# One product with four matrices of the image in place of row transform, weighting and inverse

## The chip, the cores and the metric
The kernel runs on one core of one Trainium2 chip. Time is device time in microseconds (us), the median of several runs. The core has five engines that run side by side, each with its own instruction stream in fixed order: TensorE (PE, with its weight loads PEld), VectorE (DVE), ScalarE (ACT), GpSimd (POOL), and SyncE (SP), which here only starts transfers. They wait for each other through semaphores.

## The reference, cut to what matters
32 images of 256x256 pass a three-level Haar transform, each band is weighted by a number that belongs to the image, and the inverse transform follows. A class row is put ahead, and causal attention, gates and a mixture-of-experts layer come after. The change touches the first two parts.
```python
for _ in range(3):
    cur, h, v, d = _dwt2(cur); details.append((h, v, d))        # sums and differences of pairs
aw = sigmoid(cur.reshape(B, -1) @ Wa + ba)                       # one weight of an image
rec = cur * aw[:, :, None]
for (h, v, d), (Wd, bd) in zip(reversed(details), det_params):
    w = softmax(stack([h, v, d]).reshape(B, -1) @ Wd + bd)       # three weights of an image and level
    rec = _idwt2(rec, h * w[:, 0], v * w[:, 1], d * w[:, 2])
h = concatenate([cls_tok, rec])                                  # 257 rows of 256
e = layernorm(h)
h = h + softmax(tril(e @ R @ e.T)) @ e                           # attention
h = h + ffn(layernorm(h))                                        # gates, top-k, 8 experts, scatter
```
A Haar transform along the rows of an image (over partitions) and along its columns (over the free axis) are independent of each other. Rows come in groups of 8 that don't mix in three levels.

## The kernel before, in words
**Setup** (to about 46 us): weights of the bands are laid out as images, PE forms the logits of images 0 to 15 (`logits`, the second 16 follow inside steps 0 to 2), and `mix_rows`, `mix_turned`, `mix_spread` on PE with `mix_in`, `mix_out`, `mix_columns`, `mix_table` on DVE make the table W8: for each image, row position (partition) and group of columns the weight.

**The loop over images** is a pipeline written by hand. Step t runs stage a for image t, b for t-1, c for t-2, d for t-3 and m for t-4, on every engine in the order in which its `emit` has them. Steps 0 to 7 and 28 to 35 are unrolled, 8 to 27 run as a hardware loop over four steps. There are 36 steps. In step t:
- POOL: copies of gate sums (L472, L478); then, for the statistics of b and of m, the small operations L487 to L489, the power L492 and L495 to L497 (semaphore `nrm`); then `columns` for image t+1: the column transform in three levels, L457 and L458 (level 1), L460 and L461 (level 2), L463 and L464 (level 3), which ends with semaphore `xc`; then L500.
- PE: L839 the inverse row transform of b (512 columns); L847 the turned rows of c (ET); L854 the forward row transform of a (512 columns), which waits for `xc`; L866 the turned probabilities of d; L874 the product of c with R (four products of 256 columns, "the keys' product"); L884 to L886 the probabilities times the rows of d (`av`); L894 and L896 the scores of c (`sm`).
- DVE: L1258 and L1264 statistics of the inverse's result of b (semaphore `st0`); L1272; L1279 the weights on the transformed rows of a; L1284 to L1297 the three levels of the inverse column transform; L1306 U and L1314 H1, the attention's result of d; L1321 and L1325 gate columns and row maxima of c; L1331 and L1337 statistics of H1 (semaphore `st1`).
- ACT: L634 and L636 the exponentials of d; L641 ET of c; L646 the turned probabilities of d (PTS); L650 hc, the copy of b; L614 output rows (`base_rows`); L656 GT of c; L663 the normalised rows Ex of b, after `nrm`; L671 normalised rows of m.

POOL's L487 of step t waits for `st0` of b, which DVE makes at the start of its step t, and for `st1` of m, made at the end of DVE's step t-1. PE's L854 of step t needs what POOL did in step t-1.

**After the loop** come a search for the top-k threshold (on DVE and PE) and the experts (PE), which the change doesn't touch.

Of the kernel before, what the change touches and what calls it, by code (L numbers as in the profile page):

```python
# [14 lines left out]
P = 128  # L15
# [25 lines left out]
for _name, _n in [("ident", P), ("fwd", P), ("inv", P), ("same", P), ("before", P), ("causal", P),  # L41
                  ("sign", 3), ("slot", 9), ("batch", 1), ("diag", CG), ("pick", NJ), ("spread", 4 * P),
                  ("owner", 5), ("rep1", P), ("rep2", P), ("rep3", 2 * P), ("halves", 2 * BITS)]:
    CONST[_name] = (_at, _at + _n)
    _at += _n
# [3 lines left out]
def build_program(nc, x, cls_tok, Wa, ba, Wd1, bd1, Wd2, bd2, Wd3, bd3, R, gate_w, gate_wT, gamma, beta,  # L49
                  fc1T, b1, fc2T, b2, b2T, const, out, debug=None):  # L50
    ctx = ExitStack()
    with ctx:
# [16 lines left out]
        ZP = [Hb, Ab0]  # L69
# [83 lines left out]
        def cut(n):  # L153
# [12 lines left out]
        L2 = cut(NH * 64).rearrange("p (h c) -> p h c", h=NH)  # L166
        late, a[0] = a[0], wp_end
        Zw = cut(NH * D).rearrange("p (h c) -> p h c", h=NH)
        I2 = cut(NH * 64).rearrange("p (h c) -> p h c", h=NH)
        I1 = cut(NH * 128).rearrange("p (h c) -> p h c", h=NH)  # L170
        Q = [cut(NH * D).rearrange("p (h c) -> p h c", h=NH) for _ in range(2)]
        Ex = [cut(NH * DG).rearrange("p (h c) -> p h c", h=NH) for _ in range(2)]
        assert a[0] <= late - 2 * NH * D - NH * 192
# [29 lines left out]
        W8 = sb("W8", [P, NB, 8])  # L203
# [8 lines left out]
        bw = sb("bw", [HB, 2, NJ])  # L212
        mx3 = sb("mx3", [HB, 2, 3])
        bwT = sb("bwT", [NJ, NB])
# [23 lines left out]
        names = """ld_const ld_x0 ld_x1 ld_x2 ld_x3 ld_par ld_band0 ld_band1 ld_band2 ld_band3 ld_bias ld_cls cvt wp wp_part wp_v rep lg_mm lg_m lg_r z_mm z_c z_e bw_t bw_c w8_mm w8  # L238
            cls_d cls_p cls_a cls_t et0 et_cls g_cls cls_st cls_g zero
            xc xc_l z_done zw inv q h0 st0_b st0 var pow nrm st_set hcE et et_ev er er_ev eg_ev sm nmax pexp pt pt_ev av u h1 rv  # L240
# [199 lines left out]
        def _(po):  # L440
# [9 lines left out]
            def columns(m):  # L450
# [8 lines left out]
                po.wait_ge(s["xc_l"], m.n * 2 + 1)  # L459
                g.tensor_tensor(L2[:, :, :], L1[:, :, 0::2], L1[:, :, 1::2], ALU.add).then_inc(s["xc_l"], 1)  # L460
                g.tensor_tensor(dst[:, :, 64:128], L1[:, :, 0::2], L1[:, :, 1::2], ALU.subtract)  # L461
                po.wait_ge(s["xc_l"], m.n * 2 + 2)
                g.tensor_tensor(dst[:, :, 0:32], L2[:, :, 0::2], L2[:, :, 1::2], ALU.add)  # L463
                g.tensor_tensor(dst[:, :, 32:64], L2[:, :, 0::2], L2[:, :, 1::2], ALU.subtract).then_inc(s["xc"], 1)  # L464

            def emit(t, nxt, _a, b, _c, d, m):
# [31 lines left out]
                if nxt:  # L498
                    columns(nxt)
                g.tensor_copy(TST[:, bass.ds(t.n, 1), :].rearrange("p b k -> p (b k)"), st[:, :]).then_inc(s["tab"], 1)  # L500
# [8 lines left out]
            columns(Step(0, 0))  # L509
            po.wait_ge(s["st_set"], 2)  # L510
# [78 lines left out]
        def _(act):  # L589
# [20 lines left out]
            def base_rows(m):  # L610

                after(act, f"base_st{m.p}", m.h * 16)
                for h in range(NH):
                    last = A.activation(Bs[m.p][:, h, :], H1[m.p][:, h, :], ACT.Identity,  # L614
                                        bias=N6[m.p][:, 2 + h:3 + h], scale=O1[m.p][:, h:h + 1])
                last.then_inc(s["base"], 1)

            def emit(t, _nxt, _a, b, c, d, m):
# [6 lines left out]
                if isinstance(t.n, int) and t.n == 3:  # L625
                    act.wait_ge(s["lg_mm"], 2)
                    mix_exp(1)
                if d:
# [9 lines left out]
                if c:  # L638
                    after(act, "sm", c.n - 1)
                    act.wait_ge(s["et"], c.n + 1)  # L640
                    A.activation(ET[c.p][:, :, 1:NT], Tb[:, :].rearrange("p (c t) -> p c t", c=2), ACT.Copy)\  # L641
                        .then_inc(s["et_ev"], 1)
# [4 lines left out]
                if b:  # L647
                    after(act, "h1", b.n - 3)
                    act.wait_ge(s["st0_b"], b.n + 1)
# [98 lines left out]
        def _(pe):  # L748
# [82 lines left out]
            def emit(t, _nxt, a, b, c, d, _m):  # L831
# [18 lines left out]
                if a:  # L850
# [7 lines left out]
                    if early and t.n == 3:  # L858
                        mix_turned(1)
# [814 lines left out]
```

## Time and profile before
| what | value |
|---|---|
| median of 3 runs | 832.46 us (831.77 to 833.66) |
| the profiled execution's own time | 832.74 us |
| its span, first to last instruction | 829.24 us |
| mean granted TensorE clock | 0.945 |
| loop, by the start of PE's L839: steps 5 to 32 | 90.88 to 301.12 us |
| last statistics of the loop on POOL | 325.37 us |
| search for the threshold, granted clock 340 to 380 us | 0.50 |
| experts | about 400 us to the end |

In the rows below, a timeline row gives the start in us, the duration in us, the engine, the line, the operation, what it writes and reads, its shape, the count (x2: two instructions in a row, the duration is of both; a product in fp32 is recorded as two passes) and in brackets the idle time of the engine ahead of it with what ended it. A group of a lines view gives busy time and the mean duration of one in ns. All tiles cut from ARENA have that name, and all of PSUM is `bank`.

### The profile page before, as it was taken

The numbers are of one execution on the slowest core, as the hardware profiler recorded it, in microseconds if no ns is written. First come the engines' busy times: TensorE is split into PE (matmuls) and PEld (weight loads), VectorE is DVE, ScalarE is ACT, GpSimd is POOL, SyncE is SP. The second block draws the span as 40 slices with busy tenths as digits, with TensorE's granted clock in tenths as the row PEclk, the third lists the DMA queues.
The fourth block names the chain that finished last, engine by engine and source line by source line (L and its number), as shares of the span: only waits on it lengthen the run. The fifth ranks groups of instructions, "written<-read, shape, count | busy, mean of one in ns | idle before, by whom it ended". The sixth has DMA issues, their size and how long they took to land.

```text
span 829.2 us, 15989 instructions
## 1 busy us (share of the span) xinstructions
PE 742.1 (89%) x4566; PEld 640.6 (77%) x4566; DVE 577.6 (70%) x1968; ACT 454.2 (55%) x1001; POOL 464.9 (56%) x744
## 2 busy tenths in 40 slices
PE   6988999999999984872799999999989999999994
PEld 3976667667667663761699998999989989999994
DVE  3765888888888876998878476684765856644431
ACT  1012677777777775200556665556655666566551
POOL 0155677777677755403426648467484673855533
PEclk9989999999999998555899999999999999999997
DMA  9900022122122122701213424334243352433222
GB/s 268 292 3 2 30 77 77 51 76 76 51 76 74 54 77 96 158 21 40 71 26 75 113 41 128 69 69 122 40 121 67 52 146 39 103 84 54 40 24 27
DMA packets 63570, 64.43 MB, mean 78 GB/s; under 512 B 14033, under 2 KB 57105, under 8 KB 63377
## 3 DMA queue, kind: packets, MB, share of 16 engines
q1 hardware_dynamic: 50576, 46.57, 18.7%
q0 software_dynamic: 12800, 17.12, 12.8%
q8 instruction: 26, 0.43, 0.2%
q14 instruction: 40, 0.32, 0.1%
q10 hardware_dynamic: 128, 0.00, 0.0%
HBM read 38.14 MB, written 25.53 MB: 77 GB/s over the span
## 4 chain that ended last, share of the span: by engine, by line
PE 33%; DVE 9%; issue 8%; POOL 5%; ACT 3%; DMA 2%; POOLq 0%; ACTq 0%; DVEq 0%; SPq 0%
PE bank L959 14%; PE bank L973 14%; PE bank L948 2%; DMA raw<-in_fc1T 2%; POOL w2l L517 2%; PE bank L985 1%; POOL out L553 1%; POOL yg L531 1%; ACT bank L706 1%; DVE Tc L1389 1%; DVE yl L1508 1%; DVE jk L1485 1%; PE bank L938 1%; DVE TR L1373 1%; DMA yg<-rows,idx 1%
## 5 line engine op out<-in xcount | busy, mean ns | idle before, releaser
L553 POOL DMA_INDIRECT out<-ob,sidx x72 | 114.0, 1583 | 159.4 <-ACT ob L722 145.7
L1515 DVE TENSOR_TENSOR hl<-bank,hh 128x384 fp32r<-128x384 f32 (+1 forms) x192 | 97.5, 513 | 138.5 <-ACT hh L709 134.8
L706 ACT ACTIVATE bank<-bank,b1s 128x384 f32<-128x384 f32 (+1 forms) x192 | 99.5, 518 | 137.7 <-PE bank L959 132.5
L959 PE MATMUL bank<-yh,w1h 128*128 128x384 f32 (+1 forms) x384 | 132.6, 345 | 9.5 <-DVE hl L1515 6.4
L959 PE MATMUL bank<-yh,w1l 128*128 128x384 f32 (+1 forms) x384 | 123.4, 321 | 0.0
L959 PE MATMUL bank<-yl,w1h 128*128 128x384 f32 (+1 forms) x384 | 122.9, 320 | 0.0
L973 PE MATMUL bank<-w2l,hh 128*128 128x256 f32 x384 | 108.0, 281 | 0.0
L973 PE MATMUL bank<-w2h,hh 128*128 128x256 f32 x384 | 108.0, 281 | 0.0
L973 PE MATMUL bank<-w2h,hl 128*128 128x256 f32 x384 | 107.9, 281 | 0.0
L531 POOL DMA_INDIRECT yg<-rows,idx x72 | 72.4, 1006 | 55.7 <-issue 50.6
L709 ACT ACTIVATE hh<-bank 128x384 fp32r<-128x384 f32 (+1 forms) x192 | 87.7, 457 | 6.1
L959 PEld LDWEIGHTS bank<-yh,w1h 128*128 128x128 f32 x384 | 73.8, 192 | 14.6 <-DVE hl L1515 7.8
L959 PEld LDWEIGHTS bank<-yl,w1h 128*128 128x128 f32 x384 | 73.5, 191 | 0.0
L959 PEld LDWEIGHTS bank<-yh,w1l 128*128 128x128 f32 x384 | 72.8, 190 | 0.0
L973 PEld LDWEIGHTS bank<-w2l,hh 128*128 128x128 f32 x384 | 72.6, 189 | 0.0
L973 PEld LDWEIGHTS bank<-w2h,hh 128*128 128x128 f32 x384 | 72.5, 189 | 0.0
L973 PEld LDWEIGHTS bank<-w2h,hl 128*128 128x128 f32 x384 | 72.5, 189 | 0.0
L874 PE MATMUL bank<-ET,Rw 128*128 128x256 f32 x256 | 62.4, 386 | 0.0
L874 PEld LDWEIGHTS bank<-ET,Rw 128*128 128x128 f32 x256 | 46.0, 189 | 9.7 <-issue 3.3
L894 PE MATMUL bank<-GT,ET 128*128 128x137 f32 (+1 forms) x256 | 52.5, 340 | 0.7 <-ACT GT L656 0.7
L492 POOL TENSOR_TENSOR ST<-A,mhalf 128x6 f32<-128x6 f32 x36 | 50.7, 1408 | 3.0
L663 ACT ACTIVATE ARENA<-bank,N,ST 128x256 f32<-128x256 f32 x64 | 32.6, 560 | 33.0 <-POOL O L497 33.0
(224 smaller groups left out, 1815.5 us busy)
## 6 DMA issues: line engine op xcount, KB each, us to landing
BIG<-in_x SPq DMA_DIRECT2D x4, 2048.0 KB, 16.4
out<-Bs SPq DMA_DIRECT2D x32, 256.0 KB, 2.2
rows<-Yp SPq DMA_DIRECT2D x32, 256.0 KB, 2.4
raw<-in_fc1T SPq DMA_DIRECT2D x16, 512.0 KB
raw<-in_fc2T SPq DMA_DIRECT2D x16, 512.0 KB
yg<-rows,idx POOLq DMA_INDIRECT x72, 2.9
out<-ob,sidx POOLq DMA_INDIRECT x72, 3.8
gwb<-in_gate_w SPq DMA_DIRECT2D x1, 1024.0 KB, 7.2
```

The source lines that it names most:

```text
L492: g.tensor_tensor(st[:, 8:14], A6[:, :], mhalf[:, :], ALU.pow).then_inc(s["pow"], 1)
L517: rest = g.tensor_tensor(flat(lo, half), raw[:, half * NF:(half + 1) * NF], flat(hi, half), ALU.subtract)
L531: g.indirect_dma_start(out=yg[eh][0:m, t, :], out_offset=None, in_=rows, in_offset=tok(ap=idx[eh][0:m, t:t + 1], axis=0))\
L553: g.indirect_dma_start(out=out_rows, out_offset=tok(ap=sidx[job.eh][0:m, t:t + 1], axis=0), in_=ob[t % 3][0:m, :], in_offset=None, compute ...
L663: last = A.activation(Ex[b.r][:, h, 0:D], Hb[:, h * D:(h + 1) * D], ACT.Identity, bias=N6[t.p][:, h:h + 1], scale=ST[t.p][:, 8 + h:9 + h])
L706: A.activation(h[:, 0:cur.w], h[:, 0:cur.w], ACT.Gelu_apprx_tanh, bias=b1s[:, bass.ds(cur.e, 1), f]).then_inc(s["hact"], 1)
L709: A.activation(hT[cur.p][0][:, f, 0:cur.w], h[:, 0:cur.w], ACT.Copy).then_inc(s["hhi"], 1)
L874: last = T.matmul(Rb[:, e * D:(e + 1) * D], Rw[:, j, e * P:(e + 1) * P], ET[c.p][:, j, 1:NT], start=(j == 0), stop=(j == 1))
L894: T.matmul(Sb[:, c0:c0 + w], ET[c.p][:, j, 1 + h * P:1 + (h + 1) * P], GT[c.p][:, j, 0:w], start=(j == 0), stop=False)
L959: last = T.matmul(Lb[ring(cur, f)][:, 0:cur.w], w1s[cur.eh][i][:, d, f * P:(f + 1) * P], yT[cur.p][k][:, d, 0:cur.w], start=(n == 0), stop ...
L973: mm = T.matmul(bank[4 + t % 2][:, 0:D], hT[prev.p][i][:, f, at:at + P], w2s[prev.eh][k][:, f, :], start=(n == 0), stop=(n == 23))
L1515: v.tensor_tensor(hT[cur.p][1][:, f, 0:cur.w], Lb[ring(cur, f)][:, 0:cur.w], hT[cur.p][0][:, f, 0:cur.w], ALU.subtract).then_inc(s["hlo"], 1)
```

## The change
The row transform, the weights and the inverse row transform become one linear map of the 128 rows of a column group, block diagonal in blocks of 8 rows. For each image there are four such matrices of 128x128 (index g, for the column groups; the lowest two are mixed as sum and difference so that the third column level is done inside the product as well).
- Setup: `mix_spread` is one product of 512 columns, `mix_blocks` a DVE operation of 80x512, ACT's `mix_table` copies 512 columns to OB (8x8 blocks of every image).
- POOL: `columns` has two levels instead of three. `operators` spreads the blocks of image t+1 to OP (128 x 4 x 128) by one multiplication with a mask of blocks; it stands behind `columns` and ends with semaphore `wide`.
- PE: L839 and L854 go. In stage a stand products of 2x128, 2x64, 2x64 and 2x64 columns with OP; they wait for `wide` and `xc`. The keys' product is cut in halves around L866.
- DVE: stage a copies the lowest group out of PSUM, does two levels of the inverse column transform with one operand in PSUM, writes hc, and makes the statistics of a there. The weighting and one level go.
- ACT: ET is ahead of the exponentials; the copy hc goes; L614's two halves stand around PTS; Ex reads hc.

```diff
@@ POOL
+            def operators(m):
+                after(po, "z_done", m.n - 1)
+                apart(po)
+                blocks = OB[:, bass.ds(m.n, 1), :].rearrange("p b (g k) -> p (b g) k", g=LEAF)
+                g.tensor_tensor(OP[m.p].rearrange("p g (r k) -> p g r k", k=CG),
+                                blocks.unsqueeze(2).to_broadcast([P, LEAF, P // CG, CG]),
+                                cst("blocks").rearrange("p (r k) -> p r k", k=CG).unsqueeze(1)
+                                .to_broadcast([P, LEAF, P // CG, CG]), ALU.mult).then_inc(s["wide"], 1)
...
                 if nxt:
                     columns(nxt)
+                    operators(nxt)
@@ ACT
-                if b:
-                    after(act, "h1", b.n - 3)
-                    act.wait_ge(s["st0_b"], b.n + 1)
-                    A.activation(hc[b.r][:, :, :], Hb[:, :].rearrange("p (h c) -> p h c", h=NH), ACT.Copy)
@@ PE
-                    pe.wait_ge(s["q"], b.n + 1)
-                    T.matmul(Hb[:, :], cst("inv"), Q[b.p].rearrange("p h c -> p (h c)"), start=True, stop=True)\
-                        .then_inc(s["h0"], 1)
...
-                    T.matmul(Zb[:, :], cst("fwd"), Xc[a.p].rearrange("p h c -> p (h c)"), start=True, stop=True)\
-                        .then_inc(s["z_done"], 1)
+                    T.matmul(Z[:, :, 128:256], OP[a.p][:, 3, :], X[:, :, 128:256], start=True, stop=True)
+                    T.matmul(Z[:, :, 64:128], OP[a.p][:, 2, :], X[:, :, 64:128], start=True, stop=True)
+
+                    T.matmul(Z[:, :, 0:64], OP[a.p][:, 0, :], X[:, :, 0:64], start=True, stop=False)
...
+                if c:
+                    keys(c, 0)
                 if d:
...
                 if c:
-
+                    keys(c, 1)
@@ DVE
+                    v.tensor_copy(I2[:, :, :], Z[:, :, 0:64]).then_inc(s["i4"], 1)
+                    dve.wait_ge(s["i4"], a.n + 1)
+                    v.tensor_tensor(I1[:, :, 0::2], I2[:, :, :], Z[:, :, 64:128], ALU.add)
+                    v.tensor_tensor(I1[:, :, 1::2], I2[:, :, :], Z[:, :, 64:128], ALU.subtract).then_inc(s["inv"], 1)
+                    dve.wait_ge(s["inv"], a.n + 1)
+                    v.tensor_tensor(hc[a.r][:, :, 0::2], I1[:, :, :], Z[:, :, 128:256], ALU.add)
+                    v.tensor_tensor(hc[a.r][:, :, 1::2], I1[:, :, :], Z[:, :, 128:256], ALU.subtract).then_inc(s["q"], 1)
+                    dve.wait_ge(s["q"], a.n + 1)
                     for h in range(NH):
-                        last = v.bn_stats(bn0[:, h, :], Hb[:, h * D:(h + 1) * D])
+                        last = v.bn_stats(bn0[:, h, :], hc[a.r][:, h, :])
...
-                        v.tensor_tensor(Zw.rearrange("p h (g c) -> p h g c", g=8)[:, :, g0:g1, :],
-                                        Zb[:, :].rearrange("p (h g c) -> p h g c", h=NH, g=8)[:, :, g0:g1, :], w,
-                                        ALU.mult).then_inc(s["zw"], 1)
```
POOL's stream of one step, from the last small operation on. Before (N and O are the factors that ACT waits for, ARENA the column transform, TST a table):
```order
L497 TENSOR_SCALAR O<-ST 128x2
L457 TENSOR_TENSOR ARENA<-BIG 128x256
L458 TENSOR_TENSOR ARENA<-BIG 128x2x128
L460 TENSOR_TENSOR ARENA<-ARENA 128x128
L461 TENSOR_TENSOR ARENA<-ARENA 128x2x64
L463 TENSOR_TENSOR ARENA<-ARENA 128x2x32
L464 TENSOR_TENSOR ARENA<-ARENA 128x2x32
L500 COPY TST<-ST 128x16
```
After, the same place (OB holds the blocks, C the mask):
```order
L505 TENSOR_SCALAR O<-ST 128x2
L458 TENSOR_TENSOR ARENA<-BIG 128x256
L459 TENSOR_TENSOR ARENA<-BIG 128x2x128
L461 TENSOR_TENSOR ARENA<-ARENA 128x2x64
L462 TENSOR_TENSOR ARENA<-ARENA 128x2x64
L469 TENSOR_TENSOR ARENA<-OB,C 128x512
L511 COPY TST<-ST 128x16
```
Two operations of 64 elements are gone and one of 512 stands last ahead of the table's copy.

PE's stream of one full step. Before:
```order
L839 MATMUL bank<-ARENA,C 128x512
L847 MATMUL bank<-C,ARENA 128x128 x4
L854 MATMUL bank<-ARENA,C 128x512
L866 MATMUL bank<-C,ARENA 128x128 x3
L874 MATMUL bank<-ET,Rw 128x256 x4
L884 MATMUL bank<-ARENA 128x264
```
After (ARENA alone is OP with the transformed columns, C,ARENA the identity with rows to be turned):
```order
L871 MATMUL bank<-C,ARENA 128x128 x4
L880 MATMUL bank<-ARENA 128x2x128
L881 MATMUL bank<-ARENA 128x2x64
L883 MATMUL bank<-ARENA 128x2x64
L884 MATMUL bank<-ARENA 128x2x64
L856 MATMUL bank<-ET,Rw 128x256 x2
L902 MATMUL bank<-C,ARENA 128x128 x3
L856 MATMUL bank<-ET,Rw 128x256 x2
L913 MATMUL bank<-ARENA 128x264
```
The turned probabilities (L866, now L902) stand between the halves of the keys' product.

## Rows read from the trace of the kernel before
**Rows 1.** The page: busy time, share of the span, instructions of each engine.
```profile
PE 742.1 (89%) x4566; PEld 640.6 (77%) x4566; DVE 577.6 (70%) x1968; ACT 454.2 (55%) x1001; POOL 464.9 (56%) x744
```
**Rows 2.** Timeline, PE: L839 of step 5 and of step 32.
```profile
90.88 1.12 PE L839 MATMUL bank<-ARENA,C 128*128 128x512 f32 x2 [1.34 <-ACT ARENA L663]
...
301.12 1.12 PE L839 MATMUL bank<-ARENA,C 128*128 128x512 f32 x2
```
**Rows 3.** Timeline, PE: one step inside the loop, to the next L839.
```profile
160.84 1.08 PE L839 MATMUL bank<-ARENA,C 128*128 128x512 f32 x2
...
162.33 1.12 PE L854 MATMUL bank<-ARENA,C 128*128 128x512 f32 x2
...
163.31 0.52 PE L866 MATMUL bank<-C,ARENA 128*128 128x128 f32 x3
...
163.79 1.97 PE L874 MATMUL bank<-ET,Rw 128*128 128x256 f32 x8
...
165.60 0.61 PE L884 MATMUL bank<-ARENA 128*128 128x264 f32 x2
...
166.94 0.63 PE L894 MATMUL bank<-GT,ET 128*128 128x137 f32 x4
...
168.47 1.08 PE L839 MATMUL bank<-ARENA,C 128*128 128x512 f32 x2
```
**Rows 4.** Timeline, DVE: from one L1306 to the next.
```profile
159.51 0.89 DVE L1306 SCALAR_TENSOR_TENSOR ARENA<-CX,ARENA,bank 128x264 f32<-128x264 f32 x2 [0.58 <-PE bank L886]
...
160.49 1.02 DVE L1314 SCALAR_TENSOR_TENSOR H<-ARENA,ST,hc 128x256 f32<-128x256 f32 x2
...
161.52 0.61 DVE L1325 TENSOR_REDUCE nmx<-bank 128x1 f32<-128x129 f32 x2
...
162.89 0.25 DVE L1337 BATCH_NORM_AGGREGATE ST<-bn 128x2 f32<-128x6 f32 x2
...
167.14 0.89 DVE L1306 SCALAR_TENSOR_TENSOR ARENA<-CX,ARENA,bank 128x264 f32<-128x264 f32 x2 [0.47 <-PE bank L886]
```
**Rows 5.** Timeline, ACT, the same step.
```profile
162.25 0.37 ACT L634 ACTIVATE ARENA<-bank,nmx 128x129 f32<-128x129 f32 x1 [0.75 <-DVE nmx L1325]
...
163.06 0.59 ACT L641 ACTIVATE ET<-bank 128x512 f32<-128x512 f32 x1
...
163.92 0.49 ACT L646 ACTIVATE ARENA<-bank 128x384 f32<-128x384 f32 x1 [0.27 <-PE bank L866]
```
**Rows 6.** Timeline, POOL: its next step, to the L487 after it.
```profile
164.29 0.22 POOL L487 TENSOR_SCALAR A<-ST 128x4 f32<-128x4 f32 x1 [1.60 <-DVE ST L1264]
...
167.16 0.61 POOL L457 TENSOR_TENSOR ARENA<-BIG 128x256 f32 x1
...
169.38 0.29 POOL L463 TENSOR_TENSOR ARENA<-ARENA 128x64 f32<-128x64 f32 x1
...
169.87 0.19 POOL L500 COPY TST<-ST 128x16 f32 x1
...
171.93 0.22 POOL L487 TENSOR_SCALAR A<-ST 128x4 f32<-128x4 f32 x1 [1.61 <-DVE ST L1264]
```
**Rows 7.** Timeline, DVE: L1306 in the last steps, without a stage a.
```profile
307.16 0.89 DVE L1306 SCALAR_TENSOR_TENSOR ARENA<-CX,ARENA,bank 128x264 f32<-128x264 f32 x2 [2.95 <-PE bank L886]
...
314.64 0.89 DVE L1306 SCALAR_TENSOR_TENSOR ARENA<-CX,ARENA,bank 128x264 f32<-128x264 f32 x2 [1.81 <-PE bank L886]
```
**Rows 8.** Lines by form, 150 to 300 us: L1279's two shapes.
```profile
L1279 DVE TENSOR_TENSOR ARENA<-bank,W 128x384 f32<-128x384 f32 x19 | 10.4, 548 | 0.0
L1279 DVE TENSOR_TENSOR ARENA<-bank,W 128x128 f32<-128x128 f32 x19 | 5.5, 287 | 0.7
```
**Rows 9.** L517 on POOL: duration min/median/max, first and last start.
```profile
L517 POOL TENSOR_TENSOR w1l<-raw,w1h x16: 2355/2397/2421, 336.6 to 726.3; 128x1024 fp32r<-128x1024 f32 x16
```
**Rows 10.** L1314 on DVE in the loop; then a pair and POOL's work beside it.
```profile
L1314 DVE SCALAR_TENSOR_TENSOR H<-ARENA,ST,hc x64: 477/616/928, 81.6 to 322.5; 128x256 f32<-128x256 f32 x64
...
183.88 0.83 DVE L1314 SCALAR_TENSOR_TENSOR H<-ARENA,ST,hc 128x256 f32<-128x256 f32 x1
...
183.63 0.79 POOL L458 TENSOR_TENSOR ARENA<-BIG 128x256 f32 x1
```

More of the change, by code:

```diff
@@ L40 @@
 _at = 0
-for _name, _n in [("ident", P), ("fwd", P), ("inv", P), ("same", P), ("before", P), ("causal", P),
-                  ("sign", 3), ("slot", 9), ("batch", 1), ("diag", CG), ("pick", NJ), ("spread", 4 * P),
+for _name, _n in [("ident", P), ("same", P), ("before", P), ("causal", P),
+                  ("sign", 3), ("slot", 9), ("batch", 1), ("diag", CG), ("pick", NJ), ("fold", P), ("mixed", 4 * CG), ("blocks", P),
                   ("owner", 5), ("rep1", P), ("rep2", P), ("rep3", 2 * P), ("halves", 2 * BITS)]:
@@ L608, in _, with mix_table, base_rows @@
             mix_exp(0)
[L610 to L616, printed above, removed]
+            def mix_table(i):
+                act.wait_ge(s["w8_mm"], i + 1)
+                A.activation(OB[:, i * HB:(i + 1) * HB, :].rearrange("p b k -> p (b k)"), ZP[:, :], ACT.Copy)\
+                    .then_inc(s["w8"], 1)
+            mix_table(0)
+            def base_rows(m, h):
+                if h == 0:
+                    after(act, f"base_st{m.p}", m.h * 16)
+                half = A.activation(Bs[m.p][:, h, :], H1[m.p][:, h, :], ACT.Identity,
+                                    bias=N6[m.p][:, 2 + h:3 + h], scale=O1[m.p][:, h:h + 1])
+                if h == 1:
+                    half.then_inc(s["base"], 1)
             def emit(t, _nxt, _a, b, c, d, m):
@@ L627, in emit @@
                     mix_exp(1)
+                if c:
+                    after(act, "sm", c.n - 1)
+                    act.wait_ge(s["et"], c.n + 1)
+                    A.activation(ET[c.p][:, :, 1:NT], Tb[:, :].rearrange("p (c t) -> p c t", c=2), ACT.Copy)\
+                        .then_inc(s["et_ev"], 1)
                 if d:
@@ L637, in emit @@
                                  accum_out=rsm[d.p][:, 1:2]).then_inc(s["pexp"], 1)
[L638 to L642, printed above, removed]
+                old = t.back(LAG + 1) if not isinstance(t.n, int) or t.n > LAG else None
+                if old:
+                    base_rows(old, 0)
                 if d:
@@ L673, in emit @@
                     last.then_inc(s["yp"], 1)
+                if isinstance(t.n, int) and t.n == 4:
+                    mix_table(1)
             steps(act, emit)
-            base_rows(Step(0, NB - 1))
+            for h in range(NH):
+                base_rows(Step(0, NB - 1), h)
             act.wait_ge(s["pt"], NB)
@@ L829, in _, with keys, emit @@
             last.then_inc(s["g_cls"], 1)
-            def emit(t, _nxt, a, b, c, d, _m):
+            def keys(c, e):
+                for j in range(2):
+                    last = T.matmul(Rb[:, e * D:(e + 1) * D], Rw[:, j, e * P:(e + 1) * P], ET[c.p][:, j, 1:NT],
+                                    start=(j == 0), stop=(j == 1))
+                if e == 1:
+                    last.then_inc(s["er"], 1)
+            def emit(t, _nxt, a, _b, c, d, _m):
                 early = isinstance(t.n, int) and t.n < 4
@@ L868, in emit @@
                 if c:
-                    after(pe, "er_ev", c.n)
-                    pe.wait_ge(s["et_ev"], c.n + 1)
-                    for e in range(2):
-                        for j in range(2):
-                            last = T.matmul(Rb[:, e * D:(e + 1) * D], Rw[:, j, e * P:(e + 1) * P],
-                                            ET[c.p][:, j, 1:NT], start=(j == 0), stop=(j == 1))
-                    last.then_inc(s["er"], 1)
+                    keys(c, 1)
                 if early and t.n == 3:
                     mix_spread(1)
-                    pe.wait_ge(s["w8"], 2)
+                    pe.wait_ge(s["lg_m"], 2)
                 if d:
```

144 lines of the change are left out of this document (65 added, 79 removed).

## The prediction
> **What bounds the kernel now.** I read the page first: PE is busy for 89% of the span, yet no other engine is above 70% [rows 1]. The change lies in the loop over images, so the length of a step is what counts. It comes from the starts of L839: step 5 at 90.88, step 32 at 301.12 us, 27 steps of 7.79 us on average [rows 2]. The step in the rows is one of 7.63 (160.84 to 168.47) [rows 3]; the average is higher by 0.15, since once in four steps the hardware loop turns round and costs about 0.6.
>
> Then I looked for the ring of waits that closes in one step. It begins with the attention's result: L1306 starts at 159.51, H1 at 160.49, the maxima at 161.52 [rows 4], the exponentials at 162.25 and, behind them on ACT, ET at 163.06 [rows 5]. ET lets PE begin the keys' product at 163.79; the probabilities' product follows at 165.60 and is through at 166.94 [rows 3]; L1306 starts again at 167.14 [rows 4]. That is 7.63, a step. The last three steps have no stage a and no L1279 to L1297, DVE idles 2.95 us, and they are still 7.48 us apart (307.16 to 314.64) [rows 7]: this ring alone holds them. So PE's columns and DVE's busy time are not what a step costs.
>
> A second ring takes two steps: statistics to POOL, POOL's column transform to L854, PE to L1306, DVE to the next statistics. POOL takes from L487 at 164.29 to about 169.92 (L463 at 169.38, L464 0.25 later, 0.29 long) [rows 6], PE from L854 to the end of `av` 4.61 (162.33 to 166.94) [rows 3], then 0.2, and from L1306 to the statistics that release L487 4.64 and 0.15 (167.14 to 171.93) [rows 4, 6]. Together 5.63+0.05+4.61+0.2+4.79 = 15.3 for two steps, 7.64 each: the same length. Either ring alone would hold the step.
>
> **The change, part by part.** The *first ring* loses ET and half of the keys' product. L1306 to the exponentials 2.74, to their end 0.81+0.1 (L634 at 162.25, L641 at 163.06) [rows 4, 5], to PE 0.12, the turned probabilities and their copy 1.18 (163.31 to 163.92+0.49) [rows 3, 5], to PE 0.1, `av` 1.34, 0.2: 6.6 us. In place of 7.63 it no longer binds.
>
> *PE* loses L839 and L854, 2 x 512 columns, and gains 640. A pass of L874 takes 0.22 for 256 columns (1.81 us for 8 passes, 163.79 to 165.60) [rows 3], so 512 columns are 0.9 us and 640 are 1.1, with 0.1 for the start 1.2. PE's work falls by 0.6 to about 6.6 us a step. No gain by itself.
>
> *DVE* loses L1279 and a level. With operands in PSUM 128 elements cost 0.29 and 384 cost 0.55 [rows 8], so 256 cost 0.42. The copy 0.38 with its wait, two operations of 128 0.6, two of 256 0.86, two statistics and their sum 1.01, the reciprocal 0.18: 3.0 us, in place of 4.0 (L1337 at 162.89 plus 0.25 to L1306 at 167.14) [rows 4]. DVE's whole step is 3.6+3.0 = 6.6. The statistics of a are now made a step earlier than needed, so POOL waits only for `st1`, which in these rows is ready 1.0 us before `st0` (163.14 against 164.14, 0.15 ahead of L487) [rows 4, 6].
>
> *ACT* loses one copy, of the size of L641, 0.59 [rows 5]. It is hidden behind ACT's waits before as after.
>
> *POOL* loses L463 and L464 (169.38 to 169.87, 0.49) [rows 6] and gains one operation of 512 elements. The trace has none of this shape. From below: 256 elements take 0.61 [rows 6], and at the same rate for the second 256, less the fixed part, 1.05. From above: 1024 take 2.40 [rows 9], half of it 1.2 and 1.3 with the fixed part. Of the two the longer row is nearer in kind, a stream without gaps, so I take 1.2. But L463 and L464 cost 0.245 each for 64 elements (169.38 to 169.87) [rows 6]; at that rate 512 are 2.0. I keep that as the upper end and as a rival.
> The Trainium skill ("GPSIMD Engine Reference", Performance versus the Vector engine) gives about 2.6 cycles for each element of an operation with two inputs at 1.2 GHz. An estimate from it is 1.1 us and dispatch, and the page advises VectorE for such work. The sum would stay.
>
> This operation stands ahead of `wide`, and PE's stage a waits for it. So the *second ring* gets it in full. POOL: L487 to the place of L463 5.09 [rows 6], plus 1.2 and 0.1 for wait and registers, 6.4; H1 ran beside the columns there, and without it the last two of them are some 0.4 shorter (an estimate: L458 took 0.18 more where H1 stood in its way [rows 10], and there are two), so 6.0 undisturbed. PE: 1.2 + keys 1.8 + turned 0.33 (three passes of half a 0.22) + `av` 1.34 = 4.7. DVE: L1306 to `st1` 3.63 (159.51 to 163.14) [rows 4]. Handovers 0.15+0.05+0.2. Sum 14.7, 7.35 a step, if POOL and DVE never meet.
>
> To this comes what POOL and DVE do to each other. H1 (two SBUF inputs) takes 0.48 at least, 0.62 in the median and up to 0.93 [rows 10]. The second H1, issued at 183.88 while L458 (183.63) was under way, took 0.83, and L458 took 0.79 in place of 0.61: each waited for the other. In the new ring H1 starts 5.9 us after PE's stage a begins (4.7+0.2+1.0), which with steps of 7.5 is just when POOL is at its last column operation or the new one. At worst one half of H1 (0.48) delays POOL and the new operation (about 1.0 of its 1.2) delays the other half: bounds 0 and 1.4 for two steps. The median of H1, 0.62, is nearer to no wait than to the longest; I take 0.5, for a step of **7.6**.
> The Trainium skill ("SBUF — State Buffer", Who interferes with whom) says that a DVE instruction with two SBUF inputs and a GpSimd instruction that reads SBUF exclude each other for the whole instruction. By that rule, with which the trace agrees (0.83 is 0.48 and 0.35 of waiting), rival A decides; if they only slowed each other the step would stay at the forecast.
>
> The turn of the hardware loop now touches POOL and PE but not DVE's part of the ring; I keep 0.1 of 0.15: 7.7 against 7.79 on average, 26 steps: **-2.3 us** (7.4 would give -10, 8.0 +5).
> The *last steps* have no product; there the first ring rules: two steps of 7.48 become 6.6: **-1.8**, and the step into them about **-0.5**.
> *Setup and steps 0 to 4*: the table's path gets a DVE operation of 80x512 (0.7), a product of 512 columns (0.9), a copy of 512 on ACT (0.6), and the first product on POOL (1.2), against four small copies; but it begins earlier, since `mix_blocks` stands ahead of two gate sums, and PE's stall in step 3 for the table goes while that for the blocks stays. Bounds -2 and +2; I take **-0.4**.
> Search and experts: 0, only shifted. The steps' PE share falls to about 85%; I expect the granted clock to stay full.
> Sum -5.0, on the profiled execution's 832.74 us 827.7; the median of the runs is 0.3 lower: **827.5 us**.
>
> **The rivals.**
> *A. H1 and the product exclude each other in full.* For: the pair at 183.6 [rows 10]. Against: the two find their places in time, as L458 and H1 do in most steps (0.62 in the median against 0.93). All 1.4 us count in two steps: 7.35 + 0.7 = 8.05. But a longer step moves POOL's operations away from H1 again, so I halve the excess over the forecast: 7.8, with the turn 7.9. 26 x 0.11 = +3, minus 2.7 at the two ends: 833, no change.
> *B. Slower: the operation on POOL is dear.* The place is POOL between `columns` and `wide`, with two operands that repeat. At 2.0 us the ring is 0.8 longer in two steps, 8.0, with the turn 8.1: 26 x 0.31 = +8, minus 2.7: 838. It decides from 1.6 us on (7.8 and the turn, 26 x 0.11). For: the short operations L463 and L464. Against: 2.3 ns for an element over 1024 [rows 9].
> *C. Much faster.* If H1 and POOL hardly meet and the operation takes 1.05, the step is 7.3, with the turn 7.35: 26 x 0.44 = -11.4, and -2.7: 818. For: the first ring, PE and DVE all end at 6.6, so nothing else is in the way.
> *D. The reorder on PE and ACT doesn't take ET out of the ring*, since PTS or GT come too late for `av` and `sm`. `sm` needs GT: keys end 1.4 ahead of `sm`, GT takes 0.6. Then the step stays at 7.79 and only the end gains: 831.
>
> **How the numbers follow.** Chances: forecast 0.40, A 0.17, B 0.10, C 0.23, D 0.10. The forecast's own range is 823 to 831. The range that leaves out 2 in 10 goes from 815 to 836, from C with a gain in setup to between A and B. What can be told from no change is 0.2%, 830.8 to 834.1. Faster: C, and the forecast with all but a tenth, and a little of D: 0.63. Within: most of A, half of D, the forecast's rest: 0.19. Slower: B and the rest of A: 0.18.
>
> **What would show it.** L469's mean on POOL: 1.2 us (B: 2.2). The wait ahead of PE's stage a: released by POOL in nearly every step, about 0.9 us. L1306 is released by PE and idles ahead of it. H1's pair: 1.3 us in the mean, unequal from step to step. L902 is not released by ACT's exponentials any more with long waits. The last three L1315 stand 6.6 apart. Wrong would be: a step below 7.25 or above 7.9, no wait for `wide`, or a change after the loop.

## The result, and the profile after

The changed kernel takes 836.45 us in the median of 6 runs (835.36 to 838.76), the kernel before 832.61 (831.29 to 833.66): ratio 1.0052, 95% interval 1.0034 to 1.007. It is slower by 0.5% where 827.5 us and "faster" were forecast. The profiled run took 836.97 us with a span of 835.2, against 832.74 and 829.2. From before, 3.5 us lay around that one span and from after 1.8, so the spans differ by more (6.0) than the medians (3.8). Ratios here and below leave out the few executions in a slower state, such as one of 3141 us with the early product and one of 854.7 us with the early columns.

The page, busy time of the engines (it answers to [rows 1]), and the queue that loads PE's instructions, first of the changed kernel:
```profile
PE 723.2 (87%) x4684; PEld 651.3 (78%) x4684; DVE 558.7 (67%) x1870; ACT 440.5 (53%) x971; POOL 484.1 (58%) x712
...
q8 instruction: 36, 0.59, 0.3%
```
and of the kernel before:
```profile
q8 instruction: 26, 0.43, 0.2%
```
All engines but POOL have less to do, as worked out (PE's weight loads, which overlap its products, have 10.7 us more). But ten blocks of 16 KB more are fetched on queue 8.

**In the loop** the starts of the new product of stage a, from the timeline of the changed kernel, answer to those of L839 [rows 2, 3]:
```profile
161.87 1.26 POOL L469 TENSOR_TENSOR ARENA<-OB,C 128x512 f32<-128x512 f32 x1
...
163.18 0.70 PE L880 MATMUL bank<-ARENA 128*128 128x256 f32 x2 [1.60 <-POOL ARENA L469]
...
168.09 0.89 DVE L1315 SCALAR_TENSOR_TENSOR ARENA<-CX,ARENA,bank 128x264 f32<-128x264 f32 x2 [0.73 <-PE bank L915]
168.35 1.29 POOL L469 TENSOR_TENSOR ARENA<-OB,C 128x512 f32<-128x512 f32 x1
...
169.07 1.25 DVE L1323 SCALAR_TENSOR_TENSOR H<-ARENA,ST,hc 128x256 f32<-128x256 f32 x2
...
169.86 0.60 PE L880 MATMUL bank<-ARENA 128*128 128x256 f32 x2
```
From 163.18 to 169.86 one step is 6.68 us, the next (to 178.61) 8.75: a pair is 15.43. PE waits for POOL's product in every second step only, then 1.6 us. L1315, the attention's result, starts at 82.66 for the first image and at 282.89 for the 27th: 7.70 us a step over 26 steps. Before, L1306 stood at 80.71 and 283.95: 7.82.

**At the end of the loop** the same line, DVE, where [rows 7] stood:
```profile
293.40 0.89 DVE L1315 SCALAR_TENSOR_TENSOR ARENA<-CX,ARENA,bank 128x264 f32<-128x264 f32 x2 [1.22 <-PE bank L915]
299.98 0.89 DVE L1315 SCALAR_TENSOR_TENSOR ARENA<-CX,ARENA,bank 128x264 f32<-128x264 f32 x2 [0.44 <-PE bank L915]
306.62 0.89 DVE L1315 SCALAR_TENSOR_TENSOR ARENA<-CX,ARENA,bank 128x264 f32<-128x264 f32 x2 [2.86 <-PE bank L915]
313.19 0.89 DVE L1315 SCALAR_TENSOR_TENSOR ARENA<-CX,ARENA,bank 128x264 f32<-128x264 f32 x2 [0.90 <-PE bank L915]
321.11 0.89 DVE L1315 SCALAR_TENSOR_TENSOR ARENA<-CX,ARENA,bank 128x264 f32<-128x264 f32 x2 [2.53 <-PE bank L915]
```
Three steps of 6.6 as forecast (22.83 us of before have become 19.79), but a step of 10.51 ahead of them (282.89 to 293.40; 7.86 before) and one of 7.92 behind them (6.52 before). In both the granted clock was at the half for 3.4 us. The sum from 80.71 or 82.66 on to the last image's result: setup +1.95, 26 steps -3.0, the next step +2.65, three steps -3.04, the last one +1.4. The change had nearly nothing left at that point: 321.11 against 321.16.

One profile is not enough for these parts. Two kernels of the experiments (x1 and x4, with 24 and 256 empty instructions) turned out to be the changed kernel again, and in neither did the clock fall at 287. The line in x1:
```profile
282.91 0.89 DVE L1317 SCALAR_TENSOR_TENSOR ARENA<-CX,ARENA,bank 128x264 f32<-128x264 f32 x2 [0.37 <-PE bank L915]
291.77 0.89 DVE L1317 SCALAR_TENSOR_TENSOR ARENA<-CX,ARENA,bank 128x264 f32<-128x264 f32 x2 [0.66 <-PE bank L915]
...
319.41 0.89 DVE L1317 SCALAR_TENSOR_TENSOR ARENA<-CX,ARENA,bank 128x264 f32<-128x264 f32 x2 [2.13 <-PE bank L915]
```
That step took 8.86 there and 8.84 in x4, so 1.7 of the 10.51 belong to this one execution. The fall at 317 came in all three (last step 7.51 and 7.92 in x1 and x4). The last result stood at 319.41 and 322.05 there, and at 321.85 in x2, a repeat of the kernel before: up to its last image the change gained some 0.6 us (320.9 in the mean of three traces against 321.5 of two), with single traces 2.4 ahead to 0.9 behind.

**Behind the loop**, in code that the change doesn't touch, both kernels run alike, the changed one 0.03 us ahead, until 605.8. Then PE of the changed kernel, timeline at the turn of the experts' hardware loop (where its second pass begins):
```profile
605.69 0.28 PE L988 MATMUL bank<-yl,w1h 128*128 128x260 f32 x1
605.81 0.28 PE L988 MATMUL bank<-yh,w1l 128*128 128x260 f32 x1
609.87 0.68 PE L988 MATMUL bank<-yh,w1h 128*128 128x384 f32 x1 [3.78 <-POOL w2l L530]
612.39 0.48 PE L988 MATMUL bank<-yl,w1h 128*128 128x384 f32 x1 [1.84 <-issue]
612.67 0.52 PE L988 MATMUL bank<-yh,w1l 128*128 128x384 f32 x1
```
and of the kernel before, which goes on without a gap:
```profile
605.84 0.28 PE L959 MATMUL bank<-yh,w1l 128*128 128x260 f32 x1
605.96 0.34 PE L959 MATMUL bank<-yh,w1h 128*128 128x384 f32 x1
```
Busy time by stretch (PE, its weight loads, DVE, ACT, POOL; then granted clock, DMA share, GB/s), changed kernel:
```profile
580.00:600.00 20.00, 20.00 (x158) 19.46 (x157) 13.96 (x48) 12.74 (x27) 8.09 (x8) 1.00 0.26 41
600.00:620.00 20.00, 14.26 (x85) 13.45 (x84) 11.38 (x31) 7.22 (x17) 14.73 (x10) 0.74 0.47 112
```
and before:
```profile
580.00:600.00 20.00, 20.00 (x157) 19.46 (x156) 13.93 (x48) 12.74 (x27) 8.09 (x8) 1.00 0.25 42
600.00:620.00 20.00, 17.82 (x131) 16.99 (x130) 13.75 (x36) 11.03 (x23) 17.34 (x12) 1.00 0.46 108
```
PE ran 46 products fewer in these 20 us. One wait is put down to POOL's low part of the weights, but POOL's L530 is as early as before (606.62 against 606.67), the same product of the kernel before started ahead of it (605.96), and the second wait has no releaser at all. From 604 to 700 us eight blocks came on queue 8, before none. So the 6 us by which the spans differ arise here; what had to be found is why.

### The profile page after: what moved, and what is told of

It is laid out like the page before. It is cut to its first block, busy times and chain, and to the rows that moved or that the text cites. A ratio compares the mean times of both kernels' runs of the same rounds, so it can differ in the third digit from the quotient of the medians.

```text
span 835.2 us, 15856 instructions
## 1 busy us (share of the span) xinstructions
PE 723.2 (87%) x4684; PEld 651.3 (78%) x4684; DVE 558.7 (67%) x1870; ACT 440.5 (53%) x971; POOL 484.1 (58%) x712
## 4 chain that ended last, share of the span: by engine, by line
PE 34%; DVE 8%; issue 8%; POOL 5%; ACT 3%; DMA 2%; POOLq 0%; ACTq 0%; DVEq 0%; SPq 0%
PE bank L988 15%; PE bank L1002 13%; PE bank L1014 2%; PE bank L977 2%; POOL out L566 2%; POOL w2l L530 2%; POOL yg L544 1%; DMA raw<-in_fc1T 1%; ACT bank L728 1%; DVE Tc L1398 1%; DVE yl L1517 1%; PE bank L967 1%; DVE jk L1494 1%; DVE TR L1382 1%; ACT hh L731 1%
## 5 line engine op out<-in xcount | busy, mean ns | idle before, releaser
L988 PE MATMUL bank<-yh,w1h 128*128 128x384 f32 (+1 forms) x384 | 133.2, 347 | 10.7 <-DVE hl L1524 3.8
L856 PE MATMUL bank<-ET,Rw 128*128 128x256 f32 x256 | 66.7, 383 | 1.7 <-ACT ET L652 1.7
L500 POOL TENSOR_TENSOR ST<-A,mhalf 128x6 f32<-128x6 f32 x36 | 49.0, 1362 | 3.0
L682 ACT ACTIVATE ARENA<-hc,N,ST 128x256 f32<-128x256 f32 x64 | 34.8, 593 | 29.1 <-POOL O L505 29.1
L469 POOL TENSOR_TENSOR ARENA<-OB,C 128x512 f32<-128x512 f32 x32 | 40.7, 1273 | 14.8 <-ACT OB L626 14.8
## 6 DMA issues: line engine op xcount, KB each, us to landing
BIG<-in_x SPq DMA_DIRECT2D x4, 2048.0 KB, 14.2
```

The costliest lines, as they stand in the source:

```text
L469: g.tensor_tensor(OP[m.p].rearrange("p g (r k) -> p g r k", k=CG), blocks.unsqueeze(2).to_broadcast([P, LEAF, P // CG, CG]), cst("blocks") ...
L500: g.tensor_tensor(st[:, 8:14], A6[:, :], mhalf[:, :], ALU.pow).then_inc(s["pow"], 1)
L682: last = A.activation(Ex[b.r][:, h, 0:D], hc[b.r][:, h, :], ACT.Identity, bias=N6[t.p][:, h:h + 1], scale=ST[t.p][:, 8 + h:9 + h])
L856: last = T.matmul(Rb[:, e * D:(e + 1) * D], Rw[:, j, e * P:(e + 1) * P], ET[c.p][:, j, 1:NT], start=(j == 0), stop=(j == 1))
L988: last = T.matmul(Lb[ring(cur, f)][:, 0:cur.w], w1s[cur.eh][i][:, d, f * P:(f + 1) * P], yT[cur.p][k][:, d, 0:cur.w], start=(n == 0), stop ...
```

## The experiments

Theory T1: the place of the experts' loop in PE's instructions decides whether its second pass finds them loaded. Rival R1: the clock's phase. R2: the weights from POOL. "Packets" are those of queue 8. All ratios are to the kernel before on the same chip.

**1. Empty instructions on PE** behind the loop over images:
```
             steps(pe, emit)
+            for _ in range(24):
+                pe.nop(nofuse=True)
```


> The changed kernel, with 24 empty instructions (nop) on PE between the steps and the search. Theory T1: the 6 us behind the loop are PE's instruction supply. PE's instructions come in blocks of 16 KB (queue 8), and the experts' hardware loop just fails to stay in PE's buffer when it turns round at 605.8; moved on by 24 instructions its start falls into the next block, the second pass of the loop fetches nothing (queue 8: about 27 packets in place of 36), the waits of 3.78 and 1.84 us go and the granted clock stays full at 600 to 620: 836.5 - 6.1 = 830.4. Rival R1: the clock falls by the phase of time, and the stall follows from it or from the shift: 24 instructions without work change nothing, 836.5. Rival R2: PE waits for the low part of the weights from POOL, as the profile names it: 836.5.


The kernel before got 90 of them.


> The kernel before, with 90 empty instructions on PE at the same place: by my count of instructions that is by how much the changed kernel's PE stream is longer ahead of the experts' loop. T1: the stall of the changed kernel appears in a kernel whose attention is untouched: queue 8 with 36 packets in place of 27, a wait of 4 to 6 us at about 606, half a clock behind it, 832.6 + 6 = 838.6. R1 and R2: nothing happens, 832.6 to 832.8.


And the changed kernel with 256:


> The changed kernel with 256 empty instructions at that place, a whole block of 16 KB. T1 in its exact form (the place of the loop within a block decides, not the length of the stream): the stall stays, 836.5 and about 37 packets. If only the length of the stream or a delay of some us ahead of the experts counted: another time than with 24, either a larger stall or none. The instructions themselves lie where PE waits for the gate sums (9.0 us idle ahead of the search), so they cost 0 to 1 us.


Measured: 1.003 (1.0011 to 1.0048), 1.0007 (0.9985 to 1.0028) and 1.002 (1.0001 to 1.0039), with 36, 26 and 36 packets on queue 8: as without them. The empty instructions are not in the programs that ran: the traces have as many records of PE as those of the two kernels, and 256 more of them brought no packet more, where one was expected. So these were repeats of the two kernels and tell nothing of T1. They show by how much such a ratio moves from one comparison to the next: the changed kernel stands at 1.0052, 1.003 and 1.002.

**2. Real instructions.** The same place, small products in place of the nop:
```
+            for _ in range(45):
+                T.matmul(Rb[:, 0:1], identb[:, :], causalb[:, 0:1], start=True, stop=True)
```


> The changed kernel with 45 products of one column each (bf16, 128x1, into a bank that nobody reads) on PE between the steps and the search, where it waits 9.0 us for the gate sums: 90 more instructions (weights and product each) that stay in the built program, and some 3 us of work inside that wait. T1 (the place of the experts' loop in PE's blocks of instructions): the loop's start, a few instructions ahead of a block's end, falls into the next block; the loop stays in the buffer when it turns, queue 8 shows about 27 packets, no wait of 3.8 and 1.8 us, clock 1.00 after 605: 6 us less than the changed kernel, 0.7% below it, ratio to before about 0.998. Rival R1 (the phase of the clock) and R2 (the weights from POOL): the stall stays, ratio 1.003 to 1.005.


Measured: 0.9981 (0.9961 to 1.0001), 27 packets, no wait on PE at the turn. Then the other way round, in the kernel before:


> The kernel before with 40 such products, 80 more instructions at the same place. T1: the loop moves to about where the changed kernel has it, so the stall and the refetching appear without the change: about 36 packets on queue 8, a gap of 4 to 6 us on PE at the turn of the experts' loop at about 606, half a clock behind it, ratio 1.007. R1, R2: none of it, ratio 1.000.


Measured: 1.0024 (0.9995 to 1.0053), 27 packets, no stall: a miss. The last block ahead of the turn had been fetched at 589.2.


> The kernel before with 55 small products at the same place, 110 instructions in place of 80. With 80 the last block was fetched at 589.2 us and the loop still stayed in the buffer; the changed kernel has its last fetches ahead of the turn at 585.7 and 600.1, the kernel before at 578.0 and 593.0, 7.3 us or some 110 instructions apart. T1: with 110 one more block is fetched ahead of the turn (at about 601), the loop's first block is gone, and PE stops at about 606: queue 8 with 36 packets, 5 to 6 us more, ratio 1.006 to 1.008. If the stall had another cause that comes with the changed attention: 27 packets, 1.000 to 1.002.


Measured: 1.000 (0.9986 to 1.0014), 27 packets: a miss again, though a block was now fetched at 600.5.


> The kernel before with 45 small products, 90 instructions, which by my count of the built program is exactly by how much PE's instructions ahead of the experts' loop are more in the changed kernel. 80 were too few (the last block ahead of the turn was not yet fetched) and 110 too many (a further block was fetched, at 600.5, but the loop's start then lay in the next block). T1, in the form of a block boundary: between the two both hold, the loop's first instructions lie at the end of a block that the fetching has already thrown out, and PE stops at about 606 as in the changed kernel: 36 packets on queue 8, ratio 1.006 to 1.008. If 27 packets stay here and with 98 too, the stall needs something of the changed attention beside the place, and T1 explains only its cure.


Measured: **1.0077** (1.0062 to 1.0092), 36 packets. PE at the turn, in a kernel whose attention is the old one:
```profile
607.82 0.28 PE L961 MATMUL bank<-yl,w1h 128*128 128x260 f32 x1
607.93 0.28 PE L961 MATMUL bank<-yh,w1l 128*128 128x260 f32 x1
612.27 0.52 PE L961 MATMUL bank<-yh,w1h 128*128 128x384 f32 x1 [4.06 <-issue]
612.59 0.52 PE L961 MATMUL bank<-yl,w1h 128*128 128x384 f32 x1
```
The same gap, and products at half the clock behind it (0.52 us). A second gap follows, in the next products of that line:
```profile
617.48 0.48 PE L961 MATMUL bank<-yh,w1h 128*128 128x384 f32 x1 [4.05 <-issue]
```


> The same with 49 products, 98 instructions, since my count can be off by some instructions. T1: if the loop's start is still ahead of the boundary, as with 90; if it has passed it, 27 packets and 1.000. At least one of the two must show the stall.


Measured: 1.0071 (1.0058 to 1.0085), 36 packets, one gap of 6.71 us at the turn.


> The changed kernel with only 10 small products, 20 instructions. In its trace PE ran one product after the first fetched block and then waited for the next one, so the loop's start is less than some 20 instructions ahead of a boundary. T1: 20 are enough to cure the stall, 27 packets, ratio 0.998 to 0.999 as with 45 products. If the 3 us of additional work ahead of the search or some distance in time were the cure: the stall stays, 1.003 to 1.005.


Measured: **0.9965** (0.9946 to 0.9983), 27 packets. PE at the turn:
```profile
602.88 0.28 PE L990 MATMUL bank<-yl,w1h 128*128 128x260 f32 x1
603.00 0.28 PE L990 MATMUL bank<-yh,w1l 128*128 128x260 f32 x1
603.12 0.42 PE L990 MATMUL bank<-yh,w1h 128*128 128x384 f32 x1
603.38 0.34 PE L990 MATMUL bank<-yl,w1h 128*128 128x384 f32 x1
```
So with 0, 80 and 110 instructions more the kernel before runs through, with 90 and 98 it stalls; the changed kernel, 90 longer by itself (by my count), stalls, and 20 or 90 more cure it. Neither the change's arithmetic nor a delay makes the stall: the place does. R2 falls with it, and R1 too: in the three stalled traces the clock fell 1.6 (changed kernel), 4.3 and 2.8 us behind the start of the gap, not ahead of it. How PE's store of instructions holds and drops its blocks was not looked into.

**3. The reorder.** Alone, in the kernel before (ET ahead of the exponentials, keys' halves around the turned probabilities; this is the order in a sketch, not the code):
```
 ACT: + ET copy (c)
        exponentials (d)
      - ET copy (c)
 PE:  + keys(c, 0)
        turned probabilities (d)
      - keys, both halves
      + keys(c, 1)
```


> The kernel before with the reorder alone: ET ahead of the exponentials on ACT, and the turned probabilities between the halves of the keys' product on PE. My two rings: the first one goes from 7.63 to about 6.6, the second (15.3 for two steps) stays and holds the loop at 7.7; only the last three steps, without a stage a, go from 7.48 to 6.6: -2 to -3 us, ratio 0.997. Rival: the first ring alone held the loop, and the reorder alone brings most of what the change was to bring: step 7.0 to 7.3, ratio 0.98 to 0.985. The number of PE's instructions is unchanged, so no stall behind the loop.


Measured: 1.0096 (1.0069 to 1.0123), steps of 8.07: both theories wrong. ACT and PE in one of its steps:
```profile
191.47 0.60 PE L855 MATMUL bank<-C,ARENA 128*128 128x128 f32 x4
...
192.16 0.60 ACT L631 ACTIVATE ET<-bank 128x512 f32<-128x512 f32 x1 [1.00 <-PE bank L855]
...
192.66 0.36 ACT L639 ACTIVATE ARENA<-bank,nmx 128x129 f32<-128x129 f32 x1
```
There ET waits for rows that PE turns (L855 in this kernel) only behind the 512 columns of the inverse row transform, and the exponentials stand behind ET. In the changed kernel the turned rows stand first on PE. There, undone:


> The changed kernel with the 45 products and the reorder undone: ET behind the exponentials on ACT, and both halves of the keys' product behind the turned probabilities. What the two rings of the prediction say: the first ring is back at about 7.6, while the second holds 15.4 for two steps; the step grows to 7.7 to 7.9 in the loop and to 7.5 in the three last steps: 3 to 6 us more than with the reorder, ratio 1.002 to 1.005. Rival, from the kernel before with the reorder alone, which lost 9 us: the reorder costs in the changed kernel too, and undoing it gains: ratio 0.99.


Measured: 1.028 (1.0255 to 1.0305), some 25 us above the same kernel with the reorder, far outside both. Its timeline, POOL and DVE:
```profile
202.15 0.89 DVE L1316 SCALAR_TENSOR_TENSOR ARENA<-CX,ARENA,bank 128x264 f32<-128x264 f32 x2 [1.33 <-PE bank L914]
...
203.13 1.27 POOL L469 TENSOR_TENSOR ARENA<-OB,C 128x512 f32<-128x512 f32 x1
203.13 1.95 DVE L1324 SCALAR_TENSOR_TENSOR H<-ARENA,ST,hc 128x256 f32<-128x256 f32 x2
...
210.70 0.89 DVE L1316 SCALAR_TENSOR_TENSOR ARENA<-CX,ARENA,bank 128x264 f32<-128x264 f32 x2 [1.32 <-PE bank L914]
```
The first ring is back at its 7.48 (the last three steps show it), and in each step H1 meets the new product in full: 1.95 in place of the 0.88 that it takes alone in the last steps. 7.48 + 1.07 = 8.55, the step measured. That H1's wait is the whole of the excess is read from this sum and these rows; no run took POOL's product away.

**4. Where POOL's product stands.** It is moved ahead of POOL's wait for st0 and st1:
```
+                if nxt:
...
+                    operators(nxt)
...
                 if nxt:
                     columns(nxt)
-                    operators(nxt)
```


> The changed kernel with the 24 instructions and with POOL's product for the next image (L469) moved ahead of its wait for the statistics (L495 and on), in place of behind the column transform. What bounds the changed step is the second ring, 15.4 us for two steps, and this takes 1.3 us of POOL out of it where POOL otherwise idles (0.55 and 1.62 us in every second step). Theory: up to 2.2 us less for two steps, until POOL itself (12.8 us busy of 15.4) and the first ring (6.6) hold the step: 6.8 to 7.1, 26 steps by -0.75 = -19 us: 830.4 - 19 = 811. Rival: the product now delays the normalization, and with it Ex and the turned rows on PE, and H1 meets it (exclusion of two operands in SBUF): the step stays at 7.6 to 7.7, 829 to 831.


Measured: 0.9788 (0.9752 to 0.9824), with the stall still in it (36 packets).


> POOL's product ahead of its wait for the statistics, as in the run before, and the 45 products on PE. T1: the 6 us of the stall come off the 816 of that kernel: ratio 0.971 to 0.973 in place of 0.979. R1, R2: 0.979.


Measured: **0.9742** (0.9713 to 0.9772), 811.2 us. A pair of steps takes 14.2 us (7.45 and 6.74) in place of 15.42 (168.09 to 183.51 at L1315): the 1.27 us of the product have left the ring. POOL in it:
```profile
161.26 1.28 POOL L469 TENSOR_TENSOR ARENA<-OB,C 128x512 f32<-128x512 f32 x1
...
162.62 0.22 POOL L498 TENSOR_SCALAR A<-ST 128x4 f32<-128x4 f32 x1
```
No wait for the statistics is left behind the product.


> The changed kernel with the 45 products, and with both the column transform and the product for the next image ahead of POOL's wait for the statistics (in the fast variant only the product). Theory: neither hangs on the statistics, so the second ring is cut altogether and POOL's own 6.4 us or the first ring's 6.6 holds the step: 6.6 to 6.8 in place of 7.1, 26 steps by 0.4 = 10 us below the 811 of the variant with the product alone: ratio 0.962. Rival: the normalization now waits for 3.7 us of POOL's work, Ex and Yp come later, and PE's turned rows wait: step 7.1 to 7.6, ratio 0.975 to 0.99.


Measured: 1.0137 (1.0103 to 1.0171): the rival was right, and more so than it said. Pairs of 17.1 us; ACT and PE:
```profile
191.66 1.09 ACT L681 ACTIVATE ARENA<-hc,N,ST 128x256 f32<-128x256 f32 x2 [3.25 <-POOL O L509]
...
192.90 0.63 PE L870 MATMUL bank<-C,ARENA 128*128 128x128 f32 x4 [2.22 <-ACT ARENA L681]
```
Behind this wait the granted clock fell to the half for 3.4 us, and so in each of eight pairs in a row (142.8 to 265.7 us). So part of the loss is the clock; how much, wasn't tried.

**5. The granted clock in the last steps.** PE's idle time there filled with products of 512 columns into a free bank:
```
+                if d and not c:
+                    for _ in range(2 if d.n == NB - 1 else 1):
+                        T.matmul(Zb[:, :], ident, C[:, 0:512], start=True, stop=True)
```


> The changed kernel with the 45 products and, in the two last steps (no stage a, no keys), one and two products of 512 columns on PE into a free bank ahead of its wait for the exponentials, in time that it idles (1 to 2.2 us). Theory: the fall of the granted clock at 317 to 321, which made the last step 7.92 in place of 6.5 us, comes from PE's idling there, and goes: the last step 6.5 to 6.6, 1.4 us less than the kernel with the 45 products alone (0.2%, seen in the profile rather than in the ratio). Rival: the clock falls anyway at that time, or the filling delays the turned probabilities: last step 7.9 or more.


Measured: 0.9978 (0.9965 to 0.9991). From 316 to 322 us, this kernel:
```profile
316.00:322.00 6.00, 4.88 (x59) 3.11 (x58) 4.65 (x15) 3.04 (x9) 3.80 (x10) 1.00 0.13 44
```
and the changed kernel:
```profile
316.00:322.00 6.00, 3.50 (x9) 2.16 (x9) 3.30 (x10) 3.37 (x10) 3.65 (x8) 0.72 0.26 90
```
Its last step took 6.51 us. That filling keeps the clock isn't proved by one profile: the kernel before was full there with PE busy 2.23 of 6 us. And the ratio is that of the kernel without the filling (0.9981); in this trace the clock fell at 289.0 and the step there took 10.47.


> The best of all: the changed kernel with POOL's product ahead of the statistics, the 45 products on PE against the stall, and the filling of the two last steps. The last step was 6.51 us in the fast variant without the filling already, and no clock fell there, so the filling should add nothing: 811, ratio 0.973 to 0.975. Rival: the filling saves another 1.4 us, 0.972, or delays the last steps, 0.976.


Measured: 0.9745 (0.9731 to 0.976), 811.8 us: the same as without the filling, so the early product and the instructions ahead of the search are the whole gain. The last step took 6.52 and 6.51 in the two kernels with the early product and no filling.

## Why the prediction was wrong

- **"Search and experts: 0, only shifted"** is the step that failed. It is +6 us, a shift not of time but of PE's instructions. The prediction named "a change after the loop" as a sign of being wrong, but gave it neither a price nor a chance. The kernel before with 90 instructions more shows it alone: +0.77%, 6.4 us. Without it the changed kernel is at 0.9965 with 20 instructions more and at 0.9981 with 90: 829.7 and 831.0 us, at the upper end of the forecast's own range (823 to 831). The two parts add up: -2.9 or -1.6, and +6.4, make +3.5 or +4.8 against +3.8 measured.
- **The -5.0 of the rest** came out at -1.6 to -2.9, so it is short by a second, smaller miss. In the trace of the changed kernel with 20 instructions more the last result stands 3.60 us ahead of before: setup +0.65, 26 steps -3.3, the step behind them +1.0, three steps -2.7, the last one +0.8. The 26 steps and the last three gave more than was forecast; setup, the longer step of a pair in between (8.85) and the clock in the last step took it back, as told below.
- **The step of the loop**: 7.7 forecast, 7.70 measured. L469 took 1.27 (1.2 forecast; B's 2.0 falls). H1's pair is 1.26 in the mean over 21 steps, two of 0.63 (1.3 forecast). But its way there was only half right: the wait for POOL comes in every second step, 1.6 us, since the second ring's excess is spent in one of its two steps, while the other runs at the first ring's pace. Before, 26 steps took 7.82 on this count, so the gain was 3.0 (2.3 forecast).
- **"Either ring alone would hold the step"** was too simple. The rings share DVE's H1. Undoing the reorder brought 8.55, not 7.6 to 7.7: the exclusion, which rival A gave at most 0.7 a step, cost 1.07 there. With the reorder the steps settle so that little of it is left. A itself (7.9 in this kernel) didn't come.
- **D, the reorder doesn't help**: wrong for the change (undoing it cost 25 us), right for the kernel before, where it costs 8 us. The first ring of 6.6 needs the turned rows ahead of stage a on PE, which the prediction took from the order without weighing.
- **The last steps** are 6.6 apart as said and gave -3.04 (forecast -2.3). The sum for this ring has a slip: the turned probabilities and their copy are 1.10 in its rows (163.31 to 164.41), not 1.18, which makes it 6.5.
- **Setup, -0.4**: it was +1.95 (82.66 against 80.71), at my upper bound of 2. With the same attention the first result came at 81.36 with 20 instructions more and at 85.59 with 90, where the granted clock was at the half for 3.4 and 13.7 us of the setup, in place of 6.8; so some of it is the clock. With the same 6.8 us at the half it came at 82.5 to 82.7 in three traces (the changed kernel, x1 and x3), and at 80.7 to 81.6 in the six of the old attention in its old order: 1 to 2 us are the longer setup.
- **"I expect the granted clock to stay full"**: wrong. It fell at 286.9 behind PE's wait of 1.59 for L469 (one like it stands in every second step, without a fall) and at 317.6 behind waits of 2.16 and 0.73, both times for 3.4 us. The first fall isn't the change's steady price: it came in this trace and in the one with the filling (10.51 and 10.47), not in four others of this loop, whose step took 8.84 to 8.86. The second came in all five without the filling: with it the last step took 7.3 to 7.9, in place of the 6.5 of before. Why the clock falls at one such wait and not at the next stays open.
- **C** (7.35) said that nothing but POOL's path stands in the way above 6.6, and the best variant bears that out, by another means: with the product out of the ring the step is 7.1, and the kernel 811 us.

## What to carry to other kernels

A change that alters the number of an engine's instructions moves every later loop of that engine in its instruction blocks. Where a loop behind the change shows new waits by "issue" at its turn, compare the packets of the instruction queue, and move the loop by a few instructions before judging the change. And an operation that doesn't depend on what its engine waits for belongs ahead of that wait, up to the point where the work behind it is late: the 1.3 us product moved there gained 20 us here, and the 3.7 us of product and columns together lost 13, both against the changed kernel with the 45 products. And parts of a few us that rest on one trace are worth a second one of the same program: a step of 10.51 was 8.86 there.

## What the runs showed of the hardware

- PE's instructions come in blocks of 16 KB on queue 8. A hardware loop of some 1,700 instructions by my count (1,604 of them recorded in the pass behind 499.8 us of the kernel before) turned without a fetch at the other places tried; at a window of places at least 8 and less than 30 instructions wide its second pass fetched all again: 36 packets in place of 27, and 5.6 us (changed kernel, 3.78 and 1.84), 8.1 us (90 more) and 6.7 us (98 more) without work on PE.
- The waits so caused carry "issue" (1.84, 4.06, 4.05, 6.71 us), or the name of an engine that had nothing to do with it: 3.78 us put down to POOL's L530, which ended at 608.98, 0.9 us ahead of the product.
- Behind the gap the granted clock was at the lower of its two levels, 1.2 GHz, for 10.2 us (607.7 to 618.0; with 98 more 6.8 us), which adds to the stall: a pass of 384 columns took 0.32 in place of 0.17 from start to start.
- DVE's operation with two SBUF inputs waited for POOL's product, which started with it at 203.13: the pair took 1.95 against 0.88 alone, and ended 0.7 after POOL's end at 204.40, while the product took its usual 1.27.
- The same program had its clock at the half in different places from one execution to the next: at 286.9 in one of three traces of the changed kernel, and for 13.6 us of the setup in one in place of 6.8.
- Empty instructions written on PE left no record and no packet (24, 90 and 256 of them); products of one column did, 45 in 1.27 us at the full clock.
